# Sort of the edges: unpacking on GpSimd, from a copy that ScalarE makes, with a key packed for rounding

## The reference, cut to what matters

```
h = relu(layernorm(x)); x = x + L0(h, edges, edge_attr_32, edge_type_2, edge_weight)
h = relu(layernorm(x)); x = x + L1(h, src, dst)
h = relu(layernorm(x)); x = x + L2(h, edges, edge_attr_2)
h = relu(layernorm(x)); x = x + L3(h, edges, edge_type_16)
```

## Time and profile before

| | |
|---|---|
| median of 3 runs | 4309.06 us (4308.51 to 4311.9) |
| the profiled execution | 4316.74 us |
| its span in the trace | 4315.0 us |
| busy PE / DVE / ACT / POOL | 3231.9 / 3413.9 / 2173.5 / 1715.7 us |
| the sort's loop, first to last one-hot | 1729.20 to 2179.56 us |
| granted TensorE clock, whole run | 0.89 |

### The profile page before, as it was taken

The page is one execution under the profiler, slowest core; times in us unless marked ns, Lnnn a source line. Parts: engine busy times, 40 slices in busy tenths (PEclk is TensorE's granted clock), DMA queues, the critical chain, the costliest instruction groups (busy, mean ns, idle before and its releaser), DMA issues.

```text
span 4315.0 us, 86344 instructions
## 1 busy us (share of the span) xinstructions
PE 3231.9 (75%) x31243; PEld 2713.9 (63%) x31243; DVE 3413.9 (79%) x6840; ACT 2173.5 (50%) x6347; POOL 1715.7 (40%) x2078
## 2 busy tenths in 40 slices
PE   1388888788888532566646788858799999779995
PEld 1155566556665321566645677745799999779995
DVE  5499999789999544999967878767666666779997
ACT  2366777667777222788844576630322222234443
POOL 0356677566666310000002200000455555458883
PEclk7699999999999666787877899979899999989998
DMA  4778888888888201000002211123344444213332
GB/s 91 229 221 244 241 267 265 212 242 258 259 261 259 91 15 40 8 12 11 11 10 93 80 40 41 46 94 123 112 126 125 124 128 123 89 65 128 127 129 67
DMA packets 306659, 550.64 MB, mean 128 GB/s; under 512 B 80311, under 2 KB 207993, under 8 KB 306089
## 3 DMA queue, kind: packets, MB, share of 16 engines
q1 hardware_dynamic: 252073, 380.67, 28.4%
q0 software_dynamic: 54144, 164.25, 13.6%
HBM read 433.68 MB, written 111.07 MB: 126 GB/s over the span
## 4 chain that ended last, share of the span: by engine, by line
PE 43%; DVE 37%; ACT 7%; issue 7%; DMA 3%; SPq 2%; POOL 1%; DVEq 0%; ACTq 0%; POOLq 0%
PE psum L3763 5%; PE psum L2490 4%; PE psum L3779 4%; PE psum L3714 4%; PE psum L3712 4%; DVE arena_a L1917 3%; PE psum L3679 2%; PE psum L3066 2%; PE psum L3738 2%; ACT arena_c L3029 2%; DVE arena_a L1913 2%; DVE arena_c L1925 2%; DVE arena_a L3259 2%; PE psum L2518 2%; PE psum L3351 2%
## 5 line engine op out<-in xcount | busy, mean ns | idle before, releaser
L1224 POOL DMA_INDIRECT arena_a<-src_table,src_tix x808 | 809.3, 1002 | 563.6 <-issue 387.0
L3483 POOL TENSOR_SCALAR node_hot<-arena_c 128x128 fp32r<-128x128 f32 x575 | 368.5, 652 | 902.0 <-DVE arena_c L3371 568.6
L3501 DVE SCALAR_TENSOR_TENSOR msg_parts<-psum,msg_parts 128x512 fp32r<-128x512 f32 (+2 forms) x644 | 425.6, 661 | 259.6 <-ACT msg_parts L3650 227.7
L3650 ACT ACTIVATE msg_parts<-psum 128x512 fp32r<-128x512 f32 (+2 forms) x325 | 186.4, 574 | 520.4 <-PE psum L3714 520.4
L3201 POOL TENSOR_SCALAR node_hot_dst<-arena_c 128x128 fp32r<-128x128 f32 x587 | 383.3, 670 | 122.9 <-DVE arena_c L3605 67.9
L3066 PE MATMUL psum<-arena_a,arena_c 128*128 128x150 f32 x1800 | 288.8, 330 | 174.0 <-ACT arena_c L3032 174.0
L3712 PE MATMUL psum<-arena_c,arena_a 128*128 128x128 bf16 x3675 | 406.4, 220 | 0.0
L3714 PE MATMUL psum<-arena_c,arena_a 128*128 128x128 bf16 x3675 | 406.4, 220 | 0.0
L3066 PEld LDWEIGHTS psum<-arena_a,arena_c 128*128 128x128 f32 x1800 | 283.2, 224 | 177.1 <-ACT arena_c L3032 177.1
L1408 ACT ACTIVATE arena_a<-arena_a 128x128 f32<-128x128 f32 x808 | 239.8, 298 | 254.3 <-DVE arena_a L1915 253.8
L3191 POOL TENSOR_SCALAR arena_a<-arena_a,arena_c 128x2500 bf16<-128x2500 bf16 x8 | 60.9, 7611 | 709.2 <-DMA arena_a<-bucket_lists 709.2
(11 more groups left out here) (609 smaller groups left out, 9841.2 us busy)
## 6 DMA issues: line engine op xcount, KB each, us to landing
y_rows<-arena_c SPq DMA_DIRECT2D x101, 576.0 KB, 4.1
arena_a<-bucket_rows SPq DMA_DIRECT2D x150, 384.0 KB
arena_c<-near_keys SPq DMA_DIRECT2D x101, 256.0 KB, 5.6
arena_b<-near_keys SPq DMA_DIRECT2D x101, 252.0 KB
arena_a<-bucket_rows SPq DMA_DIRECT2D x50, 448.0 KB
arena_a<-bucket_lists SPq DMA_DIRECT2D x25, 896.0 KB
pair_counts<-arena_c SPq DMA_DIRECT2D x25, 800.0 KB
arena_a<-bucket_lists SPq DMA_DIRECT2D x25, 704.0 KB
```

The source lines that it names most:

```text
L1224: e.indirect_dma_start(out_, None, table, bass.IndirectOffsetOnAxis(ap=idx, axis=0)).then_inc(sem, 16)
L3483: return e.tensor_scalar(node_hot[at % RING_M][:, i, :], iota_row, src_lo[:, b, 2 * k + j:2 * k + j + 1], None, ALU.is_equal)
L3501: e.scalar_tensor_tensor(out=to[:, 1, 0:nt, :], in0=bank[at % 4][:, 0:nt * P].rearrange("p (t f) -> p t f", f=P), scalar=0.0, in1=to[:, 0, ...
```

## The change

The unpacking leaves DVE. Three things replace it:

- ACT copies the 150 columns from PSUM to one of two SBUF tiles (`packed_copy`, signal `copied`), after the one-hot of the next block. It waits for the placing products and, from the third block on, until GpSimd has finished with that tile. PE now waits for this copy, and not for the fields, before it writes a bank again.
- GpSimd unpacks from the copy: 15 instructions for each block. It has no shifts here. Adding 2 to the 23rd to a float rounds it to an integer, so the type is found by scaling and rounding, subtracted, and the source likewise; the destination is the rest. For that, the key is packed with factors 512 and 262144 (`SRC_AT`, `TYPE_AT`).
- `pool_unpack` waits for `copied`, and at its end gives `fields`, for which PE's transposes wait as before.

One more signal, `copied`, is taken, and one more old signal is cleared for it.

```diff
-        def dve_unpack(e, own, b):
...
-            e.wait_ge(sig.packed_pe, b + 1)
-            own.step(e.tensor_copy(unpack_i[0], packed[:, 0:KT]))
-            own.mark(e.tensor_scalar(unpack_i[1], unpack_i[0], 8, None, ALU.arith_shift_right))
...
+        def pool_unpack(e, own, b):
+
             s = b % 2
+            key, attr = packed_copy[s][:, 0:KT], packed_copy[s][:, KT:3 * KT].rearrange("p (a k) -> p a k", a=2)
+            type_r, left, node_r, src_r = unpack_f
+            e.wait_ge(sig.copied, b + 1)
             if b >= 2:
                 e.wait_ge(sig.turned_pe, b - 1)
...
+            own.mark(e.tensor_scalar(type_r, key, 1.0 / TYPE_AT, WHOLE, ALU.mult, ALU.add))
+            own.step(e.tensor_copy(kept[:, 0:2, :], attr))
+            own.mark(e.tensor_scalar(left, type_r, TYPE_AT, -WHOLE * TYPE_AT, ALU.mult, ALU.add))
+            own.step(e.tensor_tensor(rest, attr, kept[:, 0:2, :], ALU.subtract))
+            own.mark(e.tensor_tensor(left, key, left, ALU.subtract))
             own.step(e.tensor_copy(kept[:, 2:4, :], rest))
+            own.step(e.tensor_scalar(node_r, left, 1.0 / SRC_AT, WHOLE, ALU.mult, ALU.add))
+            own.mark(e.tensor_scalar(f[:, TYP, :], type_r, -WHOLE, None, ALU.add))
+            own.mark(e.tensor_scalar(src_lo[:, b, :], node_r, -WHOLE, -1.0, ALU.add, ALU.add))
+            own.mark(e.tensor_scalar(f[:, SL, :], node_r, -WHOLE, -1.0, ALU.add, ALU.add))
+            own.step(e.tensor_scalar(src_r, node_r, SRC_AT, -WHOLE * SRC_AT, ALU.mult, ALU.add))
+            own.step(e.tensor_tensor(left, left, src_r, ALU.subtract))
+            own.mark(e.tensor_scalar(dst_lo[:, b, :], left, -1.0, None, ALU.add))
+            own.step(e.tensor_scalar(f[:, DL, :], left, -1.0, None, ALU.add))
             e.tensor_tensor(kept[:, 4:6, :], rest, kept[:, 2:4, :], ALU.subtract).then_inc(sig.fields, 1)
...
-            for n in range(NB + 2):
+            for n in range(NB + 1):
...
-                if n >= 2:
-                    dve_unpack(e, own, n - 2)
...
             pool_gather(e, first_of, dst_keys, begin_i[0], sig.d_keys)
+            for b in range(NB):
+                pool_unpack(e, own, b)
...
+                if 0 <= n - 2 < NB:
+                    b = n - 2
+                    e.wait_ge(sig.packed_pe, b + 1)
+                    if b >= 2:
+                        e.wait_ge(sig.fields, b - 1)
+                    e.activation(packed_copy[b % 2], bank[2 + b % 2][:, 0:3 * KT], ACT.Copy).then_inc(sig.copied, 1)
...
                     if b >= 2:
-                        e.wait_ge(sig.fields, b - 1)
+                        e.wait_ge(sig.copied, b - 1)
```

More of the change, by code:

```diff
@@ L49 @@
 NBIG = float(2.0 ** 100)
+SRC_AT, TYPE_AT, WHOLE = float(2.0 ** 9), float(2.0 ** 18), float(2.0 ** 23)
 TIME_PARTS, WEIGHT_PARTS = (0, 0, 0, 1, 1, 2), (0, 1, 2, 0, 1, 0)
@@ L294, in of_layer0 @@
                 self.q_pe, self.q_used, self.m_pe, self.m_used, self.decay_pe, self.decay_tanh, self.decay_dve,
-                self.decay_ready, self.squares, self.dist_ready, self.decayed, self.exp_rows, self.pos_ix,
+                self.decay_ready, self.decay_inverse, self.squares, self.dist_ready, self.decayed, self.exp_rows, self.pos_ix,
                 self.pos_counted, self.pos_ends, self.d_x, self.d_halves, self.d_lists, self.d_first, self.d_dst,
@@ L337, in __init__ @@
         self.flag = next(spare)
+        self.copied = next(spare)
         self.d_logits = next(spare)
@@ L701, in program @@
         tile_row = words(A_, 12015, [P, KT])
-        unpack_i = [words(A_, 12065 + i * KT, [P, KT], I32) for i in range(3)]
+        unpack_f = [words(A_, 12065 + i * KT, [P, KT]) for i in range(4)]
         attr_rest = words(A_, 11890, [P, 2 * KT])
+        packed_copy = [words(T_, s * 3 * KT, [P, 3 * KT]) for s in range(2)]
         H1 = words(A_, 0, [P, NB, D + 1])
@@ L1191, in sp_lists, with pool_constants @@
             e.wait_ge(g.d_out, 32)
-        def pool_constants(e):
-            own = Chain(e, g.pool_own)
+        def pool_constants(e, own):
             e.wait_ge(g.consts_set, 1)
@@ L2899, in dve_sort_lists @@
             own.mark(e.scalar_tensor_tensor(out=edges[:, :, 0], in0=key_i[1], scalar=32.0, in1=key_i[0], op0=ALU.mult, op1=ALU.add))
-            own.step(e.scalar_tensor_tensor(out=key_f, in0=key_i[2], scalar=256.0, in1=key_i[3], op0=ALU.mult, op1=ALU.add))
-            own.step(e.scalar_tensor_tensor(out=key_f, in0=ty_, scalar=65536.0, in1=key_f, op0=ALU.mult, op1=ALU.add))
+            own.step(e.scalar_tensor_tensor(out=key_f, in0=key_i[2], scalar=SRC_AT, in1=key_i[3], op0=ALU.mult, op1=ALU.add))
+            own.step(e.scalar_tensor_tensor(out=key_f, in0=ty_, scalar=TYPE_AT, in1=key_f, op0=ALU.mult, op1=ALU.add))
             e.wait_ge(sig.d_keys, 16)
@@ L2908, in dve_sort_lists @@
             e.tensor_copy(begin_i[1], begin[3]).then_inc(sig.start, 1)
-            e.tensor_scalar(edges[:, :, 1], key_f, 257.0, None, ALU.add)
+            e.tensor_scalar(edges[:, :, 1], key_f, SRC_AT + 1.0, None, ALU.add)
             e.tensor_copy(edges[:, :, 2:4], raw_attr_flat).then_inc(sig.listed, 1)
@@ L2950, in dve_route @@
             e.tensor_tensor(routed_v[s], bc(in_tile, 2, 3), bc(edge_in[b % RING_E][:, :, 1:4], 3, KT), ALU.mult).then_inc(sig.weighed, 1)
-        def dve_unpack(e, own, b):
+        def pool_unpack(e, own, b):
             s = b % 2
-            packed = bank[2 + s][:, 0:3 * KT]
-            e.wait_ge(sig.packed_pe, b + 1)
-            own.step(e.tensor_copy(unpack_i[0], packed[:, 0:KT]))
-            own.mark(e.tensor_scalar(unpack_i[1], unpack_i[0], 8, None, ALU.arith_shift_right))
-            own.step(e.tensor_scalar(unpack_i[2], unpack_i[0], 16, None, ALU.arith_shift_right))
-            own.mark(e.tensor_scalar(unpack_i[1], unpack_i[1], 255, None, ALU.bitwise_and))
-            own.step(e.tensor_scalar(unpack_i[0], unpack_i[0], 255, None, ALU.bitwise_and))
+            key, attr = packed_copy[s][:, 0:KT], packed_copy[s][:, KT:3 * KT].rearrange("p (a k) -> p a k", a=2)
+            type_r, left, node_r, src_r = unpack_f
+            e.wait_ge(sig.copied, b + 1)
             if b >= 2:
@@ L2964, in dve_unpack @@
             kept = attr_keep[b]
[L2965 to L2971, removed]
-            rest = attr_rest.rearrange("p (a k) -> p a k", a=2)
-            own.step(e.tensor_tensor(rest, packed[:, KT:3 * KT].rearrange("p (a k) -> p a k", a=2), kept[:, 0:2, :], ALU.subtract))
-            own.step(e.tensor_copy(kept[:, 2:4, :], rest))
+            rest = attr_rest.rearrange("p (a k) -> p a k", a=2)
+            own.mark(e.tensor_scalar(type_r, key, 1.0 / TYPE_AT, WHOLE, ALU.mult, ALU.add))
[3 more added lines that the diff above has]
+            own.mark(e.tensor_tensor(left, key, left, ALU.subtract))
+            own.step(e.tensor_copy(kept[:, 2:4, :], rest))
+            own.step(e.tensor_scalar(node_r, left, 1.0 / SRC_AT, WHOLE, ALU.mult, ALU.add))
[6 more added lines that the diff above has]
+            own.step(e.tensor_scalar(f[:, DL, :], left, -1.0, None, ALU.add))
             e.tensor_tensor(kept[:, 4:6, :], rest, kept[:, 2:4, :], ALU.subtract).then_inc(sig.fields, 1)
@@ L3006, in dve_sort, with pool_sort @@
             e.wait_ge(sig.flag, 1)
-        def pool_sort(e):
+        def pool_sort(e, own):
             pause(e)
@@ L3819, in gpsimd @@
         def gpsimd(e):
-            pool_constants(e)
+            own = Chain(e, g.pool_own)
+            pool_constants(e, own)
             sp_wait_tables0(e)
@@ L3830, in gpsimd @@
             pool_join(e, 0, 0, 1, 1)
-            pool_sort(e)
+            pool_sort(e, own)
             flag = e.value_load(all_near[0:1, 1:2], min_val=0, max_val=1)
```

## The result

| | before | changed |
|---|---|---|
| median of 7 runs each, side by side | 4311.59 us | 4299.65 us |
| lowest to highest | 4308.51 to 4317.48 | 4291.72 to 4302.03 |
| ratio | 1 | 0.9969 (0.9960 to 0.9979) |
| span of the profiled execution | 4315.0 | 4298.9 |

The change makes the kernel 12 us faster, 0.3%. The prediction said 4320, slower by a little. The time lies inside the range, but the direction was wrong.

A forecast was written before the change was run, and what follows sets the result against it. DVE alone (18.81 us a step) and the round trip (19.0) lay close together in the sort loop. A step of 19.1 gave +8.4 over 24 steps, the end +2.9, sum +11: 4320 against the median, range 4266 to 4352.

The forecast's parts named there:

- What bounds before, what goes: Sort loop: DVE alone 18.81 us a step, two-step round trip 19.0 a step; 2.24 us of DVE unpacking goes.
- DVE alone: Sort step bounded by DVE's own work: 18.81 us before, 16.6 once the 15 unpacking instructions leave.
- The trip without POOL: Round trip through ACT, PE and DVE if GpSimd's fields are ready in time: 33.8 us, 16.9 a step.
- The exclusion of DVE and POOL: Sort step: DVE and POOL exclude each other for whole instructions, at five DVE operations with two SBUF inputs.
- GpSimd is hidden: Rival for the sort loop: small POOL instructions slip between DVE's, step 16.9, time 4267; chance 0.16.
- The trip, 22.2 + U: Two sort steps: ACT 15.05, copy-to-fields latency U, transposes and prefix 1.1, route head 6.06; break-even U 15.3.
- T: Length of one sort step, 16.7 + r: forecast 19.1 us with holds, against 18.77 before.
- The price of POOL's work: GpSimd's unpacking of one block: 15 instructions and waits, 4.8 us; lower end 3.1, upper 6.5.
- r: GpSimd work left after DVE's three back-to-back operations with two SBUF inputs: 2.2 us, break-even 2.1.
- POOL's holds on DVE: Head of the route in the sort step: POOL's own holds add 0.2 us to DVE.
- The end: Pipeline's end behind the last products: 2.24 us on DVE becomes 0.35 + 4.8, so +2.9.
- rival 4: Sort loop: every POOL hold adds to DVE, 21.4 us a step, +63 and +2.9, time 4375; chance 0.05.

The follow-up runs named there:

- the prefix first: Changed kernel with PE's prefix of a block ahead of the transposes that wait for GpSimd: 4854.34 against 4893.20 for the changed kernel; rerun 4262.86 against 4307.67 before.
- ACT's early copy: Changed kernel with ACT's copy moved ahead of the large activation that ends the one-hot: 4857.68 against 4893.20 for the changed kernel, ratio 0.9929.

## Why the prediction was wrong

- **What bounds before, what goes.** This was right. DVE alone was to fall to 16.6 a step: the kernel with the prefix first shows 16.9, with 0.3 of POOL's holds. The trip without POOL was put at 16.9; ACT's early copy shows 17.1, with DVE busy for 96% of the loop, so close to its own bound.
- **The exclusion of DVE and POOL.** This was right: long waits for POOL, small ones for DVE. Of the five places that were counted POOL met four; during the scan it had no work. It turned 5.1 us of work into 14.3. The rival "GpSimd is hidden" would have given 4267 and fell; the prefix first, which makes it hidden for the trip, gives 4263.
- **The trip, 22.2 + U.** Its path was right, and one of its terms was too small. Transposes and prefix were put at 1.1 and took 1.42 on average, since PE had stood before them and in part of the blocks they ran at a granted clock of 0.50. In T this counts in full: 0.3 a step that the sum lacked.
- **The price of POOL's work.** 4.8 us forecast, 5.1 measured for a block alone. The middle of the two ends was good; the dear rows and the cheap ones were both off. The prediction's estimate from the Trainium skill, GPSIMD Engine Reference, "Elementwise — side-by-side cycle accounting", was about 3.9, and the measurement decides against it. That it led to about 4300, the measured time, is luck: it had too little work and the same wrong count of what is left.
- **r, what is left behind the block of three: this step failed.** "One instruction slips in, 0.3. r = 4.8 - 2.3 - 0.3 = 2.2." Three pass, one at each of the boundaries, because POOL's next one always stands ready when a DVE operation ends. And nine ran ahead of the block, not the seven or so that 2.3 us hold: in the block shown one at the end of the product L2937, and eight in 2.7 us beside the sum L2938 and the short operations, which do not keep POOL out (the eight take the same 2.7 alone). In the last block's rows, where POOL runs alone, the nine are 2.9 us of work, the three 1.1 and the last three 1.1. So 1.3 was left, not 2.2. The trip turns this 0.9 into 0.9 a step: about 18.2 instead of 19.1, and with a break-even at r = 2.1 it turned the sign. That 18.2 is so near the measured 18.13 is in part luck: PE's 0.3 was missing, the holds on DVE were put 0.1 too high, and the shorter steps at the loop's ends take 0.2 off the mean.
- **POOL's holds on DVE.** 0.2 in the route's head was forecast; L2934 to L2951 is 6.06 (1937.80 to 1943.86 on the timeline) against 5.94 before, so 0.12.
- **The end.** The forecast was 2.9 us, the measurement 2.3.
- **DVE becomes the bound** (rival 4, 4375): this did not happen here. It does after the prefix is moved, at 16.9 and not 21.4, since all 15 POOL instructions together hold DVE for 0.3 us a step.

The sum stood 0.35 us a step from break-even, on a remainder counted in instructions of 0.3 us. DVE's order and its boundaries were known from the rows. Taking one pass where there are three boundaries was a choice without a row.

## What to carry to other kernels

Work moved to GpSimd beside a DVE that is full of two-input operations must be priced by latency: count where in DVE's order it starts, how many boundaries it meets, and who waits for its end. If it can't be made shorter, take it off the trip: here, one reordering on PE, so that a result DVE waits for isn't queued behind a result GpSimd is late with, is worth about twice the change itself (29 us of the loop against 15). And look at what a longer wait does to the engine that waits: here, in part of the blocks, PE's matmuls behind the wait ran at a granted clock of 0.50 instead of 1.00.

## What the runs showed that I had not expected

- The exclusion is not even. POOL's 0.24 us instruction needs 5.69 us beside one DVE operation, while DVE hardly loses behind a short POOL instruction. In the block shown, POOL's instructions beside DVE's sums L2938 and L2929, which have one input, take what they take alone (L2968 0.26, L2979 0.35 on the timeline). From L2951 to the class sum it is 9.55 us after (1925.27 to 1934.82), as much as the three operations take one after the other, and the route's head grew by 0.12 for nine of POOL's.
- More DVE instructions for the same work made the kernel faster (18.14 to 17.71 a step), because their boundaries let another engine through.
- The chip on which the whole kernel took 14% longer has the same step in this loop, 18.14 and 18.13, although its granted clock over the run is 0.826 against 0.889. The first large activation starts at 2318.4 there and at 1737.3 here, so its 581 us are lost before this loop.
